# A fused graph, attention and expert layer: GpSimd's element-wise passes move to VectorE, and b_out is added in DRAM by one accumulating DMA

## The reference, cut to what matters

```
gnn : deg_out, deg_in = edge counts (at least 1)
      agg[d] = sum over edges (s, d) of xn[s] / sqrt(deg_out[s])
      h = relu((agg / sqrt(deg_in)) @ W + b);      gnn = h / max(|h|, 1e-12)
mix : q, k, v from xn @ w_qkv.T, 8 heads of 64; k and v instance-normed
      mix = (q @ (k.T @ v) / N) @ w_out.T + b_out
x1  = x + gnn + mix
ffn : layernorm(x1) -> softmax gate over 8 experts, top 1, at most 977 rows each,
      relu(row @ w1 + b1) @ w2 + b2, times the gate's probability
out = x1 + ffn
```

## Time and profile before

| | us |
|---|---|
| median of three runs | 1471.17 |
| lowest, highest | 1469.41, 1475.35 |
| span of the profiled execution, first to last instruction | 1429.1 |
| VectorE busy, whole span | 1248.9 (87%) |
| TensorE busy | 1337.7 (94%) |
| ScalarE busy | 962.9 (67%) |
| GpSimd busy | 648.8 (45%) |

### The profile page before, as it was taken

How to read it: one execution, slowest core, us unless ns; L and a number is a source line. 1 busy time by engine, 2 the same in 40 slices (tenths; PEclk the granted TensorE clock), 3 DMA queues, 4 the chain that set the end, 5 groups by cost and what they waited for, 6 DMA issues and landing times. The chain is left out here.

```text
span 1429.1 us, 43152 instructions
## 1 busy us (share of the span) xinstructions
PE 1337.7 (94%) x14715; PEld 1128.4 (79%) x14717; DVE 1248.9 (87%) x2315; ACT 962.9 (67%) x2239; POOL 648.8 (45%) x645
## 2 busy tenths in 40 slices
PE   4899999958999999999999999999998999899987
PEld 3466666637899999999999999999995788889986
DVE  7899999988789999999999999999976586867786
ACT  5588888775567767677677677676663658464754
POOL 4557663062234433334433344333331676776574
PEclk9899999988999999999999999999999999999999
DMA  9211111000011111121111121111113443353220
GB/s 299 60 42 46 54 45 39 23 31 1 4 62 50 37 37 37 37 72 38 37 37 37 37 73 37 37 37 37 41 71 104 129 139 107 102 161 95 76 77 26
DMA packets 61264, 89.57 MB, mean 63 GB/s; under 512 B 10231, under 2 KB 40591, under 8 KB 61154
## 3 DMA queue, kind: packets, MB, share of 16 engines
q1 hardware_dynamic: 50032, 67.20, 13.9%
q0 software_dynamic: 11136, 21.23, 5.3%
HBM read 62.91 MB, written 34.49 MB: 68 GB/s over the span
## 5 line engine op out<-in xcount | busy, mean ns | idle before, releaser
L1621 PE MATMUL bank<-reg_b,reg_a 128*128 128x256 f16 x4802 | 642.7, 273 | 0.7 <-ACT reg_a L1206 0.7
L1206 ACT ACTIVATE reg_a<-bank 128x392 f16<-128x392 f32 x784 | 358.8, 499 | 159.2 <-PE bank L1613 154.3
L1621 PEld LDWEIGHTS bank<-reg_b,reg_a 128*128 128x128 f16 x4802 | 428.9, 97 | 42.7 <-issue 0.9
L1860 DVE TENSOR_TENSOR reg_c<-iota_v,reg_c 128x2048 f16<-128x2048 f16 (+1 forms) x298 | 432.2, 1465 | 21.6 <-PE bank L1613 11.2
L845 POOL COPY key_deg<-deg_k 128x1 f32 (+1 forms) x49 | 105.0, 2143 | 463.0 <-DVE reg_c L1989 463.0
L1613 PE MATMUL bank<-reg_a,reg_c 128*128 128x98 f16 x3136 | 261.4, 208 | 6.1 <-DVE reg_e L2069 2.2
L1613 PEld LDWEIGHTS bank<-reg_a,reg_c 128*128 128x128 f16 x3136 | 213.5, 98 | 24.9 <-issue 7.9
L1860 DVE TENSOR_TENSOR reg_a<-iota_h,reg_c 128x1568 f16<-128x1568 f16 x196 | 215.7, 1101 | 0.0
L1816 PE MATMUL bank<-w_hi,hid_hi 128*128 128x256 f32 (+1 forms) x368 | 107.3, 292 | 12.7 <-DVE w_lo L2342 7.5
L1818 PE MATMUL bank<-w_hi,hid_lo 128*128 128x256 f32 (+1 forms) x368 | 104.6, 284 | 0.0
L1817 PE MATMUL bank<-w_lo,hid_hi 128*128 128x256 f32 (+1 forms) x368 | 104.5, 284 | 0.0
(11 more groups left out here) (360 smaller groups left out, 2529.4 us busy)
## 6 DMA issues: line engine op xcount, KB each, us to landing
reg_b<-in_L_ffn_w SPq DMA_DIRECT2D x16, 1024.0 KB
tok_rows<-reg_e SPq DMA_DIRECT2D x24, 512.0 KB, 3.8
x_t<-in_x SPq DMA_DIRECT2D x24, 256.0 KB
xnT_t<-xnT_rows SPq DMA_DIRECT2D x24, 256.0 KB, 2.9
out<-reg_e SPq DMA_DIRECT2D x24, 256.0 KB
xnT_rows<-xnT_t SPq DMA_DIRECT2D x13, 256.0 KB, 2.0
reg_a<-in_x SPq DMA_DIRECT2D x1, 3072.0 KB, 24.1
xnT_rows<-mix_hl SPq DMA_DIRECT2D x12, 256.0 KB, 2.0
```

The costliest lines, as they stand in the source:

```text
L1206: return a.activation(AT[k].rearrange("p h (w t) -> p h w t", w=2)[:, :, :, s * GROUP:(s + 1) * GROUP], tile_ps[bk][:, 0:GROUP * 2 * NB].r ...
L1621: ins = t_.matmul(agg_ps[k][:, 0:D], AT[k][:, h, :], h_all[:, h, half * D:(half + 1) * D], start=(first and h + half == 0), stop=(last and ...
L1860: return v_.tensor_tensor(out.rearrange("p t (v u) -> p t v u", u=2), iota.rearrange("p (v u) -> p v u", u=2).unsqueeze(1).to_broadcast(sh ...
```

## The change

1. A DRAM tensor `x_bias` is added. SyncE copies x into it, 6.4 MB, as 128 runs of 50,000 bytes. GpSimd then adds b_out to it by one DMA of 6250 rows of 1024 bytes, whose source is the same row each time. The loads of x for the pairs read `x_bias` and wait for that DMA. GpSimd's L888 goes.
2. `block_keys` of GpSimd becomes `keys` on VectorE: two integer instructions as before, one `scalar_tensor_tensor` and one copy of 128x64.
3. ScalarE's `agg_evac` and GpSimd's L896 become one VectorE instruction a block, `scaled` (128x256 from PSUM, times two factors), and L900 becomes `biased` on VectorE (128x512 a pair).
4. GpSimd has no arithmetic left between `h_part` and the experts.

```diff
+        sp.dma_start(x_bias.rearrange("(p j) d -> p (j d)", p=XB_ROWS), x.rearrange("(p j) d -> p (j d)", p=XB_ROWS)
+                     ).then_inc(xb_in, 16)
         sp.dma_start(gate_w_sb[:, :, :], gate_w.rearrange("(c p) d -> p c d", p=P)).then_inc(w_in2, 16)
...
-            sp.dma_start(x_t[:, :, :], pair_rows(x, q)).then_inc(x_ld, 16)
+            sp.dma_start(x_t[:, :, :], pair_rows(x_bias, q)).then_inc(x_ld, 16)
...
         sp.wait_ge(hw_ready, NB)
+        sp.wait_ge(xb_set, 16)
         load_pair(0)
...
-        pool.wait_ge(degin_set, 3)
-        block_keys(0, 0)
+        pool.wait_ge(xb_in, 16)
+        g.dma_start(x_bias[:, :], b_out.rearrange("(a d) -> a d", a=1).to_broadcast([N, D]), accum_op=ALU.add
+                    ).then_inc(xb_set, 16)
         pool.wait_ge(deg_ok, 1)
         pool.wait_ge(hw_out, H_POOL[-1] + 1)
-        h_part(H_POOL[:6])
-        block_keys(1, 1)
-        h_part(H_POOL[6:])
+        h_part(H_POOL)
...
-        def key_halves(b):
+        def keys(b, k):
             apart(dve)
             src_b = slot_src[:, ds(b, 1), :].rearrange("p a j -> p (a j)")
             v_.tensor_scalar(key_i[:, 0, :], src_b, P - 1, None, ALU.bitwise_and)
             v_.tensor_scalar(key_i[:, 1, :], src_b, 7, None, ALU.logical_shift_right).then_inc(key_int, 1)
+            dve.wait_ge(key_int, b + 1)
+            apart(dve)
+            v_.scalar_tensor_tensor(key_t[k][:, 0, :], iota_k[:, :], deg_k[:, ds(b, 1)], key_i[:, 0, :], ALU.subtract, ALU.max)
+            v_.tensor_copy(key_t[k][:, 1, :], key_i[:, 1, :]).then_inc(key_set, 1)
...
+        def scaled(b, k):
+            out_ = last_fin.g[:, 0, :] if fixed(b, NB - 1) else g_s[:, k, :]
+            dve.wait_ge(agg_done, b + 1)
+            apart(dve)
+            v_.scalar_tensor_tensor(out_, agg_ps[k][:, 0:D], rin[:, ds(b, 1)], norm_bc[:, :], ALU.mult, ALU.mult
+                                    ).then_inc(agg_out, 1)
+
+        def biased(q):
+            w, gs = blocks_of(q), fin_of(q).g
+            dve.wait_ge(agg_out, q * 2 + (w + 2))
+            apart(dve)
+            v_.tensor_tensor(gs[:, 0:w, :], gs[:, 0:w, :], gnn_b_bc[:, :].unsqueeze(1).to_broadcast([P, w, D]), ALU.add
+                             ).then_inc(fin_scaled, 2)
...
         def first(q, c):
             w, o = blocks_of(q), fin_of(q)
+            if c == 0:
+                scaled(q * 2 + 1, 1)
             if c == 1:
+                biased(q)
...
-            dve.wait_ge(x_added, q + 1)
+            dve.wait_ge(x_ld, (NQ + 2) * 16 if fixed(q, NQ) else (q + 1) * 16)
...
             if c == 0:
+                if not isinstance(q, int) or q < NQ - 1:
+                    dve.wait_ge(fin_relu, q + 1)
+                    scaled(q * 2 + 2, 0)
```

More of the change, by code:

```diff
@@ L107 @@
 XB = 6
+XB_ROWS = 250
 ROWS_LATE = {1: 2, 2: 3}
@@ L127, in build @@
     tok_rows = dram("tok_rows", (NPAD, TOKW))
+    x_bias = dram("x_bias", (N, D))
     early = ExitStack()
@@ L234, in build @@
     bd_sb = reg_e[:, 2048:2560].rearrange("p (c d) -> p c d", c=IC)
-    agg_s, g_s, relu_h, mixed = (reg_e[:, k * 2 * D:(k + 1) * 2 * D].rearrange("p (m d) -> p m d", m=2)
-                                  for k in range(4))
+    g_s, relu_h, mixed = (reg_e[:, k * 2 * D:(k + 1) * 2 * D].rearrange("p (m d) -> p m d", m=2) for k in range(1, 4))
     tok_t = reg_e[:, 2048:2048 + 2 * TOKW].rearrange("p (m d) -> p m d", m=2)
@@ L271, in build @@
     in_sd, rin = sb("in_sd", [P, NB]), sb("rin", [P, NB])
-    x_idx, key_deg = sb("x_idx", [P, 1], I32), sb("key_deg", [P, 1])
+    x_idx = sb("x_idx", [P, 1], I32)
     x_at, x_next = sb("x_at", [P, 1]), sb("x_next", [P, 1])
@@ L443, in build @@
     last_fin = Finish(
-        one(D), halves(place_of(D)), one(D), one(D), one(D), one(D), one(TOKW), halves(reg_c[:, 0:D]),
+        one(D), halves(place_of(D)), one(D), one(D), one(D), one(TOKW), halves(reg_c[:, 0:D]),
         halves(reg_c[:, D:2 * D]), [place_of(D)], *(place_of(1) for _ in range(6)), [place_of(6)], one(2),
@@ L626, in pair_rows @@
             if blocks_of(q) == 1:
-                n = LAST if rows is x or rows is out else P
+                n = LAST if rows is x_bias or rows is out else P
             rows = rows[ds(first, n), :]
@@ L874, in gnn @@
         def gnn(b, k, fin, with_rounds=True):
[L875 to L901, removed]
-        def tail():
[L904 to L909, removed]
-        main_phase(pool, gnn, lambda b, s: None, lambda q, s: first(q), lambda q, s: None, tail)
+            if with_rounds and not fixed(b, 0):
+                more(b - 1, rounds_of(pool, b - 1))
+        def tail():
+            more(NB - 1, rounds_of(pool, NB - 1))
+        main_phase(pool, gnn, lambda b, s: None, lambda q, s: None, lambda q, s: None, tail)
         pool.wait_ge(agg_done, NB)
@@ L1207, in tile_evac @@
                                 tile_ps[bk][:, 0:GROUP * 2 * NB].rearrange("p (t w h) -> p h w t", w=2, t=GROUP), ACT.Copy)
-        def agg_evac(b, k):
-            if not fixed(b, 0) and not fixed(b, 1) and not fixed(b, NB - 1):
-                act.wait_ge(fin_scaled, b - k)
-            act.wait_ge(agg_done, b + 1)
-            apart(act)
-            agg = last_fin.agg if fixed(b, NB - 1) else agg_s
-            a.activation(agg[:, k, :], agg_ps[k][:, 0:D], ACT.Copy, scale=rin[:, ds(b, 1)]).then_inc(agg_out, 1)
         def more(b, k, rounds):
@@ L1233, in gnn @@
                 act.wait_ge(deg_ok, 2)
-            if not fixed(b, 0) and not fixed(b, 1):
-                agg_evac(b - 2, k)
             for s in range(SLOTS):
@@ L2018, in keys_begin @@
             dve.wait_ge(slots_in, 16 * NB)
-            key_halves(0)
             dve.wait_ge(base_set, 4)
             dve.wait_ge(consts, 20)
+            dve.wait_ge(degin_set, 3)
+            keys(0, 0)
             dve.wait_ge(deg_ok, 1)
@@ L2045, in late_pair @@
                 rounds()
-                dve.wait_ge(key_set, 1)
-                key_halves(1)
+                keys(1, 1)
             if q < NQ:
@@ L2116, in gnn @@
                 if c == 1 and not fixed(b, NB - 1) and not fixed(b, NB - 2):
-                    dve.wait_ge(key_set, b + 2)
-                    key_halves(b + 2)
+                    dve.wait_ge(key_ready, b + 1)
+                    keys(b + 2, k)
                 fin(c)
@@ L2133, in prepare @@
         def prepare(b, c):
+            if (b, c) == (2, 0):
+                scaled(0, 0)
             if (b, c) == (1, 1):
@@ L2278, in tail @@
             link(v_.tensor_scalar(node_1[:, NB - 1:NB], node_1[:, NB - 1:NB], valid[:, :], None, ALU.mult))
-            first(NQ - 1, 1)
-            first(NQ - 1, 3)
+            for c in (0, 1, 3):
+                first(NQ - 1, c)
             for c in (0, 1):
@@ L2284, in tail @@
             more(NB - 1, last_rounds)
-            last_scaled()
+            scaled(NB - 1, 0)
+            biased(NQ)
             first(NQ, 3)
```

32 lines of the change are left out of this document (6 added, 26 removed).

## The result

The changed kernel takes 1534.68 us, the median of four runs (1526.21 to 1539.34), beside 1470.29 us for the kernel before: ratio 1.0431, 95% interval 1.039 to 1.0471. It is slower by 64 us. The forecast was 1475 us, no measurable change, within 1466 to 1502.

The account below looks back on a forecast made before the run. TensorE was taken to bound the main phase, VectorE almost a co-bound. Main phase 0, copy +5, accumulating DMA 0, entry −0.3, tail −0.5 sum to +4.2 us; with 1429.1 + 42.1 that gives 1475 us, range 1466 to 1502.

Parts of the forecast that it names:

- two deadlines: Accumulating DMA: GpSimd may be held 73 us after issue, until 318; the landing may take 130 us, until 375.7.
- 0 us, hidden by the rest of the kv phase: Accumulating DMA: taken as 63.5 us from its issue at 245.5, costing nothing, with 10 us to spare.
- The rival of the late DMA: kv phase: accumulating DMA on 10 of 16 engines takes 102 us, holds GpSimd, first sums 29 us late; chance 0.22.
- the rule that the prediction cites: DMA: a transfer uses the largest number of engines up to 16 dividing its slowest dimension; for 6250 rows, 10.
- Forecast +5: Start of kv phase: the copy of x delays the first store that `high_T(1)` needs; +5 us, bounds 0 and +23.
- 0.53 x 4: Ahead of the copy: queue share used to estimate that the old loads last from 36 until about 38 us.
- a delay of up to 0.7 us each is smaller than the lead of up to four chunks in the ring: Main phase: TensorE's ring absorbs the delays from `biased`, the second block's `scaled` and the masked keys; 0 us.
- stand ahead of the next one-hot tiles: Main phase, VectorE's queue: `biased`, the second block's `scaled` and the masked keys delay these tiles, up to 0.7 us each.
- VectorE becomes the bound: Main phase: new operations cost twice their rows, need 31.6 to 32.5 us a pair against 30.46; 1487 us, chance 0.04.
- Forecast −0.3 and −0.5: Entry: two key makings added, TensorE's 0.62 us wait gone, −0.3; tail: GpSimd's passes leave VectorE's routing, −0.5; each ±1.
- The 42.1 us: Whole kernel: the median's excess over the profiled span of 1429.1 us, taken as unchanged by the change.
- All three signs of being wrong: `h_part` starting after 318; the pair's period over 0.3 us off 30.46; time beside the span other than 42 us.

Follow-up runs that it names:

- r13: The change's VectorE moves alone, x loaded from x, b_out added in SBUF by one accumulating DMA a pair; ratio to the kernel before 1.0066.
- r12: The changed kernel itself, run again on one chip with its parts; ratio to the kernel before 1.0438.
- r3: The changed kernel with the copy of x but without the accumulating DMA, b_out not added; 1489.37 us.
- r8: The changed kernel with its DMAs swapped: SyncE fills x_bias with b_out, GpSimd's accumulating DMA adds x in 800 runs of 8000 bytes; 1567.42 us, ratio 1.0646.
- r11: The changed kernel with its accumulating DMA behind GpSimd's `h_part` instead of ahead of it; 1508.22 us, ratio 1.0545.
- r2: The changed kernel without its two DMAs, x loaded as before and b_out not added; 1482.14 us, ratio 1.0112 to the kernel before.
- r4: The kernel before with the two DMAs and without L888; keys, norm and bias stay on GpSimd; 1511.34 us, ratio 1.0323.
- r5: r2 with VectorE's keys moved behind the low half (L2178); 1474.31 us, ratio to the kernel before 1.0016.
- r7: r2 with both keys and `scaled` moved behind the low half (L2178); 1467.91 us, ratio to the kernel before 0.9981.
- r14: The changed kernel with keys and `scaled` behind the low half (L2178), nothing else changed; ratio to the kernel before 1.0268.
- r1: The kernel before, unchanged, traced a second time; 1464.84 us, ratio 1.0004.
- r15: The kernel before with the two DMAs alone, run again beside the changed kernel; ratio 1.0358.
- r10: r7 with b_out added to the pair's x in SBUF by one accumulating DMA a pair; 1422.54 us, ratio to the kernel before 0.9946.

## Why the prediction failed

**The accumulating DMA (the largest error).** I took 63.5 us, a price of GpSimd's issuing, for both the hold and the landing, and called it hidden, with two deadlines, GpSimd's queue and the landing. GpSimd was held for 4.30 us, and the landing took 110.9, inside the bounds of 17.4 and 161. But neither deadline was where it cost: the 130 us for the landing sufficed in the changed kernel. The step that failed is "0 us, hidden by the rest of the kv phase": that phase is not only cover, it stores every pair through the same 16 DMA engines and reuses the buffer once the store has landed. Between r13 and r12, 44.4 us lie ahead of block 0; 7 of them are the copy's (r3), some 37 the held stores'; ScalarE's waits for stores add up to 40.1 us there (r12, 280 to 405 us), and r13 has none. That r8's short accumulation holds hardly any store, and r11's, placed behind them, none, shows it.

The rival of the late DMA had the sign and a good part of the size (+29) by a wrong mechanism, so that its 102 us beside the measured 110.9 are luck: it had GpSimd held all the time by 10 of 16 engines. From 280 to 410 us GpSimd's queue kept 81.4% of the time of 16 engines busy:

```profile
q0 software_dynamic: 6474, 6.60, 81.4%
```

Ten engines with one transfer at a time could make 62.5% at most. So I infer that more than 10, and most likely all 16, were at work, and that the rule that the prediction cites does not hold for this DMA, but the exception that it names beside it. The Trainium skill ("DMA: Bandwidth & Descriptors", section "Queues, rings and completion order") says that each DMA engine takes turns between queues by whole packets, about 9 to 17 descriptors each. The trace doesn't contradict it and doesn't test it: the store issued at 292.94 released ScalarE at 311.41, and whether the length of the turns is what makes these 18.5 us was not tried.

**The copy.** Forecast +5, measured +7.2 (r3 less r2), with its wait at the place named. It takes 26 to 28 us from issue to landing (r3, r4, r11, r12), and the issue is at about 29.5 us, so it lands near 57 against the forecast 55.5; the 17.4 us counted from 38, behind the backlog. One reading there is wrong without effect: the 0.53 in "0.53 x 4" is the clock's column of the earlier trace rows, and the GB/s give 180 / 367 = 0.49.

**Main phase, VectorE.** I compared amounts: 28.7 to 29.6 us of work against a period of 30.46, so 0 us. The amounts were right (about 3 us came, 3.2 went; one-hot tiles at 1.22 and 0.97). That the busy share fell to 90%, where I had it stay near 95%, is no contradiction: part of what came is handoff, in which VectorE isn't busy. My sentence "a delay of up to 0.7 us each is smaller than the lead of up to four chunks in the ring" was right for one-hot tiles, which are finished 6 to 11 us before TensorE's builds begin to read them. It was applied to the wrong consumer. The step that failed is "stand ahead of the next one-hot tiles": they also stand ahead of the low half L2178, and that has no ring. Before, L2241 to the end of L2211, which are the same two instructions, ran from 600.41 to 610.39, 9.98 us:

```profile
609.70 0.69 DVE L2211 SCALAR_TENSOR_TENSOR reg_c<-reg_e,reg_c 128x512 f16<-128x512 f32 x1
```

With the other 20.32 us of the loop that is 30.30, just under the 30.38 of a full TensorE; now, with 10.93 us, it is 31.25, over it. The 3.2 us freed lie ahead of the slot matmuls, where VectorE can only wait (1.1 us); the 0.95 us are added behind them. This cost 16.6 us in blocks 4 to 48. Runs r5 to r7 and r14 show it. The rival "VectorE becomes the bound" had 12 us from an excess of work that does not exist.

**Entry and tail.** Forecast −0.3 and −0.5. The entry gives back 3 to 7 us (60.8 against 67.4 in r2 and r1, 62.2 against 65.5 in r12 and r15). r1 shows a 2.8 us wait of TensorE for GpSimd's keys there, where the earlier trace rows had 0.62, and it is gone; the rest was not traced to one cause. The tail is within 3 us, unresolved.

**The time beside the span.** The 42.1 us were no constant: in r1 and in the changed kernel 1 us lies between a run's time and its span. I put the rest down to the chips, since the kernel before takes 1431 us on one of them; which one the first trace came from isn't recorded. It made no error in the ratio.

All three signs of being wrong came: `h_part` after 318 (386.22, but behind the long kv phase and not behind the DMA's issue), a period more than 0.3 us off (31.25), and another time beside the span.

## What to carry to other kernels

A phase whose DMA engines are nearly idle (a busy share of 0.16 and less from 100 to 300 us before the change) is still no cover for a long DMA, if stores of that phase gate its buffers: list who waits for other transfers while it runs. Price such a DMA from a run with the same pieces, source and operation, not from its bytes: the same 6.4 MB landed in 35.8 or 110.9 us. Work moved to an engine with time to spare must be placed by the consumer that has the least slack, not by the total: look for the pair of waits (A for B once a turn, B for A once a turn) that marks a latency loop, and put additions behind its last product. Time freed ahead of the loop's entry is lost; here 3.2 us a pair were.

## What the runs showed of the hardware

- An accumulating DMA in DRAM of 6250 rows of 1 KB took 110.5 to 117.0 us in all its runs, with stores beside it and without, at 58 GB/s; in 8 KB pieces 35.8 us (179 GB/s). GpSimd was free after 4.30 and 1.39 us. The two differ in their source too, so the size of the pieces is not shown to be the only cause.
- 256 accumulated rows of 1 KB from SBUF into SBUF took 3.8 us to landing (r10), that is 16 x 3.8 / 256 = 0.24 us a row on each of 16 engines, with all fixed time in it.
- While the accumulating DMA ran and no store did (r11), TensorE waited 26.4 us for "issue" in blocks 0 to 4, against 1.7 us in r10.
- SyncE's queue stood 88.77 us behind a plain DMA of 6250 rows of 1 KB from one repeated row (r8), and it issued nothing meanwhile; ScalarE waited 83.3 us for the first store. Behind the copy of the same bytes in 128 runs the next instruction of the queue went out after 1.02 us.
- The same kernel takes 1431 or 1464 to 1471 us on different chips, and between the two traces of it 29 of 32 us lie in the kv phase, with TensorE waiting for "issue" (15.7 us from 100 to 300 us in r1).
